# Attention with a routed feed-forward on one core: scatters moved ahead of the last power, the shared weights' split moved to other engines, the slot table cut in three, less warming

## What is computed

```python
def xattn(q, k, v):                       # q = layernorm(x), k = v = ctx
    scaled = einsum('bsd,bse->bde', q, k) / sqrt(256)
    attn = softmax(scaled, axis=1)
    return einsum('bde,bse->bsd', attn, v)

x = x + xattn(layernorm(x), ctx, ctx)
xf = layernorm(x)                         # called z below
y, g = split(xf @ shared_gw.T)
shared = silu(g) * y @ shared_dw.T
scores = sigmoid(xf @ gate_w.T)
topk_idx = top_k(scores + gate_bias, 2)   # weights: scores at topk_idx, summed to 1
out = sum over the 8 experts of (silu(g_e) * u_e) @ down_w[e].T * w_e
x = x + shared + out
```

## Time and profile before

| | us |
|---|---|
| median of 3 runs | 245.96 |
| lowest and highest of them | 245.94, 248.5 |
| the profiled execution | 246.86 |
| its span, first to last instruction | 245.1 |

### The profile page before, as it was taken

One profiled execution on the slowest core, in us unless ns is written; L12 is line 12 of the kernel. 1 busy time (PEld: TensorE's weight loads), 2 busy tenths in 40 slices (PEclk: granted clock), 3 DMA queues, 4 the chain that ended last, 5 costly groups with the idle time before them and its releaser, 6 DMA issues.

```text
span 245.1 us, 5588 instructions
## 1 busy us (share of the span) xinstructions
PE 214.3 (87%) x1533; PEld 188.5 (77%) x1533; DVE 164.9 (67%) x617; ACT 129.8 (53%) x406; POOL 128.0 (52%) x179
## 2 busy tenths in 40 slices
PE   7676999899999999699469998999999999999900
PEld 7444767677677999599359997999999999899800
DVE  2646586997987597956235598777777776335870
ACT  3645699987875424131134755665666666314700
POOL 4538387687666477787000443444444444503890
PEclk9998899999999999799957999999999999999995
DMA  5898757699111033233211434444444442179541
GB/s 175 276 288 250 248 151 222 209 268 275 63 48 45 27 114 114 94 114 112 71 45 48 134 90 135 132 136 132 138 134 135 133 136 88 67 263 424 173 150 43
DMA packets 25598, 36.15 MB, mean 147 GB/s; under 512 B 5248, under 2 KB 20352, under 8 KB 25184
## 3 DMA queue, kind: packets, MB, share of 16 engines
q1 hardware_dynamic: 22160, 26.22, 35.0%
q0 software_dynamic: 3408, 9.57, 10.7%
HBM read 22.02 MB, written 13.75 MB: 146 GB/s over the span
## 4 chain that ended last, share of the span: by engine, by line
PE 53%; POOL 14%; issue 10%; DVE 6%; ACT 6%; DMA 5%; SPq 3%; POOLq 1%; DVEq 0%; ACTq 0%
POOL slot_rows L453 9%; PE bank L950 9%; PE bank L952 8%; PE bank L951 8%; PE bank L976 4%; PE bank L1093 4%; PE bank L965 3%; DMA sul_raw<-shared_upT 3%; PE bank L1119 3%; PE bank L1043 3%; ACT att L563 2%; PE bank L1131 2%; PE bank L1060 2%; PE bank L1136 2%; PE bank L1135 2%
## 5 line engine op out<-in xcount | busy, mean ns | idle before, releaser
L517 POOL DMA_INDIRECT expert_out<-att,yi x39 | 37.3, 955 | 59.9 <-ACT att L529 59.9
L453 POOL DMA_INDIRECT slot_rows<-z_all,desti x32 | 32.6, 1018 | 8.8 <-issue 8.8
L563 ACT ACTIVATE att<-bank,nb 128x256 f32<-128x256 f32 x64 | 29.3, 473 | 3.2 <-DVE nb L699 3.2
L950 PE MATMUL bank<-uph,xh 128*128 x78 | 29.5, 378 | 1.4 <-DVE xl L898 0.8
L950 PE MATMUL bank<-zTh,suh 128*128 128x256 f32 (+1 forms) x96 | 30.6, 319 | 0.0
L952 PE MATMUL bank<-zTh,sul 128*128 128x256 f32 (+1 forms) x96 | 27.8, 290 | 0.0
L951 PE MATMUL bank<-zTl,suh 128*128 128x256 f32 (+1 forms) x96 | 27.8, 289 | 0.0
L1043 PE MATMUL bank<-sd,s_hm 128*128 128x256 f32 (+1 forms) x96 | 24.4, 393 | 2.1 <-DVE x_all L821 2.0
L951 PE MATMUL bank<-upl,xh 128*128 x78 | 26.0, 333 | 0.0
L952 PE MATMUL bank<-uph,xl 128*128 x78 | 25.8, 331 | 0.0
L898 DVE TENSOR_TENSOR xl<-bank,xh 128x256 fp32r<-128x256 f32 x39 | 16.5, 424 | 12.8 <-ACT xh L529 12.6
(11 more groups left out here) (136 smaller groups left out, 596.3 us busy)
## 6 DMA issues: line engine op xcount, KB each, us to landing
cr<-slot_rows SPq DMA_DIRECT2D x39, 136.0 KB, 2.1
y_all<-expert_out SPq DMA_DIRECT2D x3, 1024.0 KB, 8.7
upl_raw<-up_wT SPq DMA_DIRECT2D x8, 352.0 KB, 3.5
cr<-ctx_kv SPq DMA_DIRECT2D x16, 128.0 KB, 3.5
crT<-ctx_kvT SPq DMA_DIRECT2D x16, 128.0 KB, 2.5
dnl_raw<-down_wT SPq DMA_DIRECT2D x8, 256.0 KB, 3.7
out<-x_all SPq DMA_DIRECT2D x16, 128.0 KB, 1.7
x_all<-x SPq DMA_DIRECT2D x1, 1024.0 KB, 7.8
```

The lines of the kernel that those rows point to most:

```text
L453: nc.gpsimd.indirect_dma_start(slot_rows, bass.IndirectOffsetOnAxis(ap=desti[:, k, t:t + 1], axis=0), z_all[:, t, :], None).then_inc(sent, 16)
L517: nc.gpsimd.indirect_dma_start(expert_out, bass.IndirectOffsetOnAxis(ap=yi[:, t:t + 1], axis=0), ys[t % 3], None).then_inc(y_out[t % 3], 16)
L563: last = nc.scalar.activation(att[:, j, m:m + D], ps_s[j][b][:, c * D:(c + 1) * D], ACT.Exp, bias=nb[:, j, n:n + 1], accum_out=rs[:, j, n: ...
L950: mm(o, ah, bh, start=(n == 0), stop=False)
```

## The change

- FILL goes from 4 to 2.
- The high half of the shared weights is copied by ACT at the end of its steps 1 and 2 (`copy`, as for `uph`), no longer by DVE in steps 0 and 1. POOL's `shared_low` moves to steps 2 and 3, behind `values` and ahead of `deviations`.
- `SEND_STEP` takes one scatter in steps 10, 11, 12 and 14, two in steps 13 and 15, three in step 16: 11 in all. In every step they now stand ahead of `deviations`, in step 16 too. 21 are left for after the loop.
- `slot_table` is cut into `slot_counts` (step 22), `slot_starts` (step 23) and `slot_table` (step 24), each behind DVE's piece of that step.
- Piece 15 uses Silu and one DVE operation, like the late pieces. `shared_add(7)` is done behind piece 14, no longer behind piece 15.

```diff
--- before.py
+++ after.py
@@ -218,7 +218,7 @@
             return 0 <= t < NT
 
         WARM = 10
-        FILL = 4
+        FILL = 2
 
 
         XG = [(0, 1), (1, 2), (2, 4), (4, 8), (8, 16)]
@@ -234,12 +234,14 @@
 
         def sending():
 
+            halves = [(t, k) for t in range(NT) for k in range(K)]
             at = []
-            for a, b in BATCHES:
-                for t in range(a, b):
-                    for k in range(K):
-                        at.append((max(b + 6, at[-1][0] + 1 if at else 0), t, k))
-            return [(p, t, k) for p, t, k in at if p <= NT], [(t, k) for p, t, k in at if p > NT]
+            for p in range(BATCHES[0][1] + 6, NT + 1):
+                for i in range(3 if p == NT else 2 if p in (NT - 3, NT - 1) else 1):
+                    t, k = halves.pop(0)
+                    assert p >= [b for a, b in BATCHES if a <= t < b][0] + 6
+                    at.append((p, t, k))
+            return at, halves
 
         SEND_STEP, SEND_LATER = sending()
 
@@ -488,21 +490,19 @@
             for p in STEPS:
                 if live(p):
                     values(p)
+                if 2 <= p < DC + 2:
+                    shared_low(p - 2)
                 if up_split(p - 1) is not None:
                     expert_low(up_split(p - 1))
-                if not live(p) and (live(p - 1) or live(p + 3)):
-                    deviations(p)
                 for at, t, k in SEND_STEP:
                     if at == p:
                         scatter(t, k)
-                if live(p):
+                if live(p - 1) or live(p + 3):
                     deviations(p)
                 if p == -3:
                     prepare()
                 if p == -2:
                     gate_split()
-                if 1 <= p < DC + 1:
-                    shared_low(p - 1)
                 if p == -1:
                     z_tails()
                 if p == 0:
@@ -534,7 +534,7 @@
                     act.wait_ge(sup_done, n + 1)
                     if n >= 2:
                         act.wait_ge(shm_done, n - 1)
-                    if n in EARLY:
+                    if n < PAUSE - 1:
 
                         nc.scalar.activation(s_sg[0:m, n % 2, :], gu(n)[0:m, 0:GN], ACT.Tanh,
                                              scale=0.5).then_inc(ssg_done, 1)
@@ -601,6 +601,9 @@
                     normalised(p - 1)
                 if p > NT:
                     from_z_bank(p)
+                if 1 <= p < DC + 1:
+                    act.wait_ge(sw_in, 16)
+                    copy(suh[:, p - 1, :], su_raw[:, p - 1, :]).then_inc(sw_high, 1)
                 if up_split(p) is not None:
                     expert_high(up_split(p), False)
                 if down_split(p) is not None:
@@ -760,7 +763,7 @@
                 link(nc.vector.tensor_reduce(sbias[:, t, 0:K].rearrange("p t k -> p k t"), hit[:, :, t, :], AX.X, ALU.add))
                 nc.vector.tensor_copy(desti[:, :, t], sbias[:, t, 0:K].rearrange("p t k -> p k t")).then_inc(dest_done, 1)
 
-            def slot_table():
+            def slot_counts():
 
                 link(nc.vector.tensor_copy(count[:, :], rank[:, NT * E:(NT + 1) * E]))
                 link(nc.vector.tensor_tensor(big[:, :, :], count[:, :].unsqueeze(2).broadcast_to([P, E, NT]),
@@ -770,6 +773,8 @@
                                              ntile[:, :].unsqueeze(1).broadcast_to([P, E, E]), ALU.mult))
                 link(nc.vector.tensor_reduce(first[:, :], tri[:, :, :], AX.X, ALU.add))
 
+            def slot_starts():
+
                 nc.vector.tensor_tensor(start[:, 0:E], count[:, :], ebase[:, :], ALU.add).then_inc(count_done, 1)
                 link(nc.vector.tensor_tensor(behind[:, :], ntile[:, :], first[:, :], ALU.add))
                 link(nc.vector.scalar_tensor_tensor(start[:, 0:E], behind[:, :], -float(P), start[:, 0:E],
@@ -777,6 +782,8 @@
                 link(nc.vector.tensor_tensor(jump[:, :], start[:, 1:E + 1], start[:, 0:E], ALU.subtract))
                 link(nc.vector.tensor_tensor(past[:, :, :], tileno[:, :].unsqueeze(2).broadcast_to([P, SLOTS, E]),
                                              behind[:, :].unsqueeze(1).broadcast_to([P, SLOTS, E]), ALU.is_ge))
+
+            def slot_table():
                 link(nc.vector.tensor_tensor(leap[:, :, :], past[0:1, :, :],
                                              jump[0:1, :].unsqueeze(1).broadcast_to([1, SLOTS, E]), ALU.mult))
                 nc.vector.tensor_reduce(eslot[:, :], past[:, :, :], AX.X, ALU.add)
@@ -807,22 +814,19 @@
                     if n % SC == 0 and n // SC >= 2:
                         dve.wait_ge(sdn_done, GT * (n // SC - 1))
                     g, u = gu(n)[0:m, 0:GN], gu(n)[0:m, GN:2 * GN]
-                    if n in EARLY:
+                    if n < PAUSE - 1:
                         link(nc.vector.scalar_tensor_tensor(s_sg[0:m, n % 2, :], s_sg[0:m, n % 2, :], 1.0, u, ALU.add, ALU.mult))
                         nc.vector.scalar_tensor_tensor(h, s_sg[0:m, n % 2, :], 0.5, g,
                                                        ALU.mult, ALU.mult).then_inc(shm_done, 1)
                     else:
                         nc.vector.tensor_tensor(h, s_sg[0:m, n % 2, :], u, ALU.mult).then_inc(shm_done, 1)
-                for t in DOWNS.get(n - 1, []):
+
+                for t in (DOWNS.get(n - 1, []) if n != PAUSE - 1 else []) + (DOWNS[n] if n == PAUSE - 2 else []):
                     shared_add(t)
 
             def shared_add(t):
                 dve.wait_ge(sdn_done, t + 1)
                 nc.vector.tensor_tensor(x_all[:, t, :], dn(t), x_all[:, t, :], ALU.add).then_inc(sacc_done, 1)
-
-            def shared_high(piece):
-                dve.wait_ge(sw_in, 16)
-                nc.vector.tensor_copy(suh[:, piece, :], su_raw[:, piece, :]).then_inc(sw_high, 1)
 
             def down_low(e):
                 dve.wait_ge(dn_high, e + 1)
@@ -879,11 +883,13 @@
                 if after(p):
                     shared_piece(after(p) - 1)
                 routing(p)
-                if 0 <= p < DC:
-                    shared_high(p)
                 if down_split(p - 1) is not None:
                     down_low(down_split(p - 1))
                 if batch(p - 1, 2) == len(BATCHES) - 1:
+                    slot_counts()
+                if batch(p - 2, 2) == len(BATCHES) - 1:
+                    slot_starts()
+                if batch(p - 3, 2) == len(BATCHES) - 1:
                     slot_table()
 
                     dve.wait_ge(sc_done, B2 * NT)
```

## The result

The changed kernel takes 235.52 us, the median of 4 runs (233.37 to 237.1), against 245.95 (245.75 to 248.5) for the kernel before: a ratio of 0.952, 95% interval 0.941 to 0.964. The ratios in this document leave out executions more than 1.5% above the fastest of their kernel, here the one of 237.1 us, while the medians keep them; the two medians give 0.958. The forecast was 231.4 us in 227.5 to 236. The direction, the range and most steps held; the point was 4.1 us too low. Its profiled execution took 234.21 us with a span of 232.5, against 246.86 and 245.1: 12.6 us of span are gained where 14.6 were forecast. That is 1.9 us of the miss.

What follows compares the result with a forecast made beforehand. No engine bounds the whole kernel; the chain runs over the start's transfer, POOL's scatters and the hand-over. T(0), PE's first turn of expert rows, 9.3 us sooner plus 5.3 makes 14.6 off 246.86: 232.3, median 231.4 us, range 227.5 to 236.

Steps and rivals of the forecast that it cites:

- Part 1: Kernel start: moving the shared weights' split to ACT and later on POOL gains 3.4 us, between 0 and 4.6.
- Rival C: Start: gains only 0 to 1 us, as ACT's wait costs what DVE's did; 234.3 us, chance 0.1.
- Rival A: Start: the clock doesn't fall there; 1.2 us better, 230.2 us, chance 0.2.
- Part 2: Attention, `attend(4)` to `attend(15)`: half the filling saves 2.0 us, bounds 0 and 5.8.
- Part 3: Attention's end: more scatters sent early; last power's product ends 3.1 us sooner, last scatter starts at 106.2 instead of 115.87.
- Rival B: Ahead of T(0): PE stands 2 us or more, then runs at half clock; 234.8 us, chance 0.2.
- Part 4: PE's work before T(0): cutting the slot table gives about 2.6 us, pieces come 3.1 sooner; PE ready at 112.2.
- Part 5: Hand-over, T(0) to fourth product up: full clock and no wait for `shared_add`, 7.5 instead of 12.82 us, gain 5.3.
- rival D: Hand-over: Silu's table load with a drain holds ACT 2.7 us; 232.8 us, chance 0.1.
- Rival E: Attention: half the filling lets the clock fall repeatedly, about 3 us lost per step, up to about 279 us; chance 0.03.
- F: Whole kernel: nothing moves the end, as the scatters slow each other down; 245 to 246 us, chance 0.02.

Runs made afterwards that it cites:

- the first section: The first measurement and profile of the changed kernel, nothing further edited, against the kernel before: 235.52 against 245.95 us, ratio 0.952.
- group 1: Chip of the follow-ups on the start and the filling: changed kernel unaltered 244.61 us, kernel before 255.89, ratio 0.954.
- group 2: Chip of the follow-ups on scatters, slot table and hand-over: changed kernel unaltered 237.13 us, kernel before 247.27, ratio 0.955.
- group 3: Chip of the follow-ups on PE's wait ahead of piece 3: changed kernel unaltered 244.57 us, kernel before 256.56, ratio 0.955.

## Why the prediction held, and where it missed

**Part 1, the start: right number, other limiter.** 3.4 us of gain were forecast, 3.32 came (31.25 to 27.93); undoing the edit moved `attend(4)` by 2.0. But ACT did not stand waiting for the transfer, which the forecast had it do. This time it landed 6.8 us after its issue instead of 8.0, at 14.2, and ACT's copy came right behind `q`. ACT's timeline:

```profile
13.77 0.60 ACT L576 ACTIVATE q<-x_all,nm,rstd 128x256 f32<-128x256 f32 x1
14.27 0.79 ACT L529 ACTIVATE suh<-sul_raw 128x704 fp32r<-128x704 f32 x1
...
16.23 0.47 ACT L563 ACTIVATE att<-bank,nb 128x256 f32<-128x256 f32 x1 [1.18 <-DVE nb L702]
```

What then held the exponentials of tile 2 until 16.23 was PE: its scores ran at half clock (8 products in 1.81 us, above) behind a wait of 2.96 us. The forecast had this start at 16.2 too, for the wrong reason, and that part of the match is luck. It put the wait ahead of `attend(0)` at 2.3 and one half-clock spell behind it; the wait was longer, and the spell came where it was put. Rival C (nothing gained at the start) is out. Rival A (no fall) did not happen in this execution, but it is real: the run with the table whole has the same start, a wait of 2.24 us, a clock of 1.00 and `attend(4)` at 26.41, where the forecast had 26.7 without a fall. PE's row:

```profile
11.68 1.09 PE L980 MATMUL bank<-att,vT 128*64 128x256 f32 x8 [2.24 <-POOL vT L480]
```

How much of the 3.32 is the earlier landing and how much the edit was not separated.

**Part 2, the filling: the term that was mis-sized.** 2.0 us were forecast from `attend(4)` to `attend(15)`, 0.5 came (45.94 to 45.43), and FILL = 4 gave the same 0.5 back. The forecast compared the engines' mean shares and took PE's, at 26.90 of 28 us, for a part of the step. But of those 26.90 the filling was work that stood in a gap: PE runs it while it would wait for `vT` in any case. With half of it gone, PE is busy for 23.15 of 28 us and waits instead. The rows fit a loop over two steps that sets the pace; which operations close it was not tested. `attend` starts at intervals of 4.41 and 3.87 us in turn (27.93, 32.34, 36.21), 8.3 us together; the earlier trace rows have 12.50 us from 31.25 to 43.75 for three steps, 8.3 for two. The short gaps ahead of `attend` name POOL's `vT`:

```profile
32.34 1.09 PE L982 MATMUL bank<-att,vT 128*64 128x256 f32 x8 [0.76 <-POOL vT L480]
...
36.21 1.09 PE L982 MATMUL bank<-att,vT 128*64 128x256 f32 x8 [0.21 <-POOL vT L480]
```

This is 1.5 us of the 1.9 missing in the profile. The other 0.4 is the gather, which held T(0) for 0.37 us behind PE's own end.

**Part 3, the scatters: right, but for the price of the wait.** `attend(15)` to the end of the last product took 8.27 us (8.1 forecast), from there to the last scatter 25.83 (26.3), and PE's wait ahead of piece 3 was 2.20 ("some 2 us"). From the last scatter's start to T(0) it took 6.78, 1.1 more than the 5.66 carried over and 0.8 more than the forecast's 112.2 needs; 0.44 of it stands in the last scatter itself (1.40 us, before 0.96). What was missing is the clock behind that wait. In the first section's profile it stayed up, so the 1.9 us hold nothing of this; it bears on the median. Rival B had the mechanism (2 us or more of standing, then half clock) but only ahead of T(0). It came at piece 3, in four of the eight profiles that have this wait, for 1.5 us (group 1) to 2.6 us (group 2). The step that failed is the one that wrote "PE will stand some 2 us" and priced nothing behind it, with 2.10 and 2.04 us in the earlier trace rows as waits behind which the clock had fallen.

**Part 4, PE's own end: the size held, the reason by half.** PE was ready at 114.24 - 0.37 = 113.87 instead of 117.9, 4.0 us sooner. The pieces came 1.4 sooner, where 3.1 were forecast: that is part 2's shortfall. What is left by subtraction is 2.6, as forecast for the table. The wait went from 2.04 to 1.00 (1.2 forecast). But only about 1.0 of the 2.6 is the cut's own; for the rest the clock had to stay up, and with the table in one piece, in group 2, it stayed up too. So it isn't shown that the cut is what kept it up. The two ends met as said, with 0.37 us between them, so rival B's wait ahead of T(0) didn't appear.

**Part 5, the hand-over: right.** 5.3 us were forecast. T(0) to the first result scatter went from 134.74 - 121.53 = 13.21 to 122.25 - 114.24 = 8.01, 5.2 us; in the forecast's own landmark, the fourth product up, it is 12.82 to 7.42 (121.66). The 7.5 written there is a slip that happened to fit: its terms, 3.2 and two slots at 2.0, add up to 7.2. Tanh put back costs 2.4 of the 5.2, and most of the rest fits the clock: with only the scatters put back, and so a wait of 6.21 us ahead of T(0), this stretch took 2.0 us longer. The table load is where the forecast put it. ACT's timeline, with the earlier trace rows for before:

```profile
115.09 1.28 ACT L542 ACT_TABLE_LOAD   x1
116.39 0.38 ACT L542 ACTIVATE s_sg<-bank 128x256 f32<-128x256 f32 x1
```

Silu starts 0.02 us behind the load's end, so rival D is out. ScalarE: Activation LUTs, section What ACT_TABLE_LOAD costs, in the Trainium skill has the load's time right; its drain of 1.38 us is not to be seen here, on an ACT that had just ended a copy.

**The rest.** The first result scatter to the 39th takes 200.41 - 122.25 = 78.2 us after and 213.09 - 134.74 = 78.4 before: the experts' stage is unchanged, as said. Rival E did not come true at half the filling, where the clock of the attention's windows is 0.94 to 1.00, but its spells come singly in step 8, and the run without filling shows how near it is; F is out.

## What to carry to other kernels

Work put in to keep an engine warm stands in its gaps: its cost need not be its busy time. Here halving it took some 3 us of PE's work out of 28 (26.31 to 23.27 in group 1) and gave 0.5 in the whole attention, and it brought waits behind which the clock fell in some executions. Whether an engine's queue sets the pace is better seen in the intervals of one landmark over several steps than in busy shares. When work is moved to a sooner place in a queue, price the wait that it makes there with the clock that may fall behind it, even if the wait itself is off the path. And gains that meet at one point, here PE's own end, the scatters and the hand-over at T(0), pay only together: undoing the scatters alone made PE stand for 6.2 us again.

## What was not expected of the hardware

**The same wait, the clock up or down.** Eight profiles have PE's wait ahead of piece 3, of 2.19 to 2.23 us. In four the granted clock fell behind it from 2.4 to 1.2 GHz: for about 7 us in the three of group 2 (2.19, 2.21 and 2.19) and for about 3 us in group 1's unaltered kernel (2.23). In the other four it stayed up: 2.20 in the first section, 2.22 and 2.19 in group 1, 2.22 in group 3. Behind 1.98 us it stayed up, behind 2.04 us it had fallen; behind 1.36 or 1.37 us in step 8 of the attention it fell in four profiles of nine; and behind 3.02 us ahead of `attend(0)`, in the run with the split as before, it stayed up. So no length of the wait parts the two here, and nothing in the profiles says which it will be. Each fall costs 1.5 to 2.6 us, the size of the gaps between executions of one kernel.

**On two chips PE and ACT stall during the scatters.** In groups 1 and 3 both kernels are slower: the one before takes 255.9 and 256.6 us against 246 and 247.3 in the first section and group 2, the changed one 244.6 and 244.6 against 235.5 and 237.1. Timeline of PE in group 1's unaltered kernel; "issue" is waiting for nothing that the profile shows:

```profile
95.03 0.17 PE L1011 MATMUL bank<-both,below 128*128 128x8 bf16 x1 [1.10 <-issue]
...
97.82 0.17 PE L1011 MATMUL bank<-both,below 128*128 128x8 bf16 x1 [1.90 <-issue]
99.25 0.17 PE L1014 MATMUL bank<-both,ones 128*128 128x8 bf16 x1 [1.26 <-issue]
```

From 92 to 100 us PE is busy for 2.65 of 8 us, while POOL sends its scatters; in group 2's unaltered kernel it is busy for all 8. Then POOL has to wait itself, for row numbers that the stalled engines were to make, and during that wait they go on:

```profile
97.61 0.96 POOL L455 DMA_INDIRECT slot_rows<-z_all,desti  x1 [0.30 <-issue]
102.21 0.96 POOL L455 DMA_INDIRECT slot_rows<-z_all,desti  x1 [3.64 <-DVE desti L764]
```

All eight profiles of these two chips have this pair: a wait of POOL for `desti` of 3.6 to 5.2 us, and PE going on within 3 us of its start. No profile of the first section or of group 2 has either. It looks as if PE and ACT get their instructions late while indirect transfers run back to back; scatters spaced out would test it, which wasn't tried, and why it shows on some chips only stays open.

**The same transfer took 5.7 to 8.0 us.** The 704 KB of shared weights landed 8.0 us after their issue in the profile before, 6.8 after, and 5.7 to 7.1 in the other twelve, so a bound that rests on one landing time is loose by 2 us.
